# GpSimd weight products in four parts, and four early row normalisations on ScalarE instead of VectorE

## The chip, the cores and the metric

One core of one Trainium2 chip. The metric is the device time of one launch in microseconds, the median of the runs shown; lower is better.

## What is computed

Two layers on x (32 batches of 256 rows of 512 numbers), with a context of the same shape. The first works on a layer norm of x, three products with 256x256 weights and a grouped normalisation; the second is a gated feed-forward layer of width 1408 whose inputs and weights are rounded to 4-bit floating point in blocks of 16.

```python
def fp4_quant_dequant(x):                      # blocks of 16 along the last dim
    scale = max(max|x| of the block / 6, 1e-12)
    q = _GRID[searchsorted(_MID, |x / scale|)] * sign(x) * scale

x = x + xattn(layernorm(x), ctx, ctx, Wt, Wp, Wg, Wz, gamma, beta)
xn = fp4_quant_dequant(layernorm(x))
gate, y = xn @ fp4(w_gate).T, xn @ fp4(w_up).T
x = x + fp4_quant_dequant(silu(gate) * y) @ fp4(w_down).T
```

## The kernel before

Each batch b has two tiles of 128 rows (t = 2b + s). After a prologue, a hardware loop on every engine (`Fori(1, NB - 2)`) handles one batch per turn; the last batches are written out. Each engine executes its own list of instructions in the order in which the builder's functions are called, and engines meet only through semaphores. So an instruction that waits holds everything that its engine has queued behind it. Nothing but these lists, written out by hand, sets the order.

The prologue rounds the three feed-forward weights. A weight is four chunks of 128x1408 numbers (88 blocks of 16), 12 chunks n = 0 to 11 in all. For each chunk VectorE finds block maxima (`weight_max`) and scales (`weight_scales`); GpSimd multiplies the chunk by the inverse scales (`weight_y`, L1848); ScalarE makes a rounding grain (`weight_grain`, L915); VectorE adds and takes away the grain (`weight_round`, L1470 and L1473); GpSimd multiplies by the scales (`weight_q`, L1856). TensorE then transposes the chunk in 34 sets (`turn_weights`, L597), ScalarE copies each as float16 (`weights_hi`, L938), TensorE forms the remainder (`turn_again`, L605 and L607), ScalarE copies that (`weights_lo`, L944).

Woven into this are batches 0 and 1. `ln1(b)` on GpSimd makes the inverse deviations of layer norm 1, `root2(t)` that of layer norm 2. `normalise1(b, s)` (VectorE, L1223) and `normalise2(t)` (VectorE, L1272) apply them: `(x - mean) * rstd` on 128x512 numbers. ScalarE's `q_hi(b)` (L910) copies the normalised x_in as float16, GpSimd's `q_lo` (L1802) makes the remainder, SyncE's `turn_c`, `turn_q` transpose by DMA in that order, and TensorE's `gram(b)` (L500) takes both. `columns(0)` (L1810 and on) and `columns_affine(0)` (L1821 to L1831) are small GpSimd operations on the way to ScalarE's `affine` (L859), VectorE's `residual` (L1258) and `x1_mean` (L1266).

On the path of a tile's second layer, VectorE runs `x_first` (block maxima, L1205), `x_scales` (L1208, L1283), `x_y` (L1184), ScalarE `grain_x` (L915), VectorE `x_add`, `x_back`, `x_quant`, ScalarE `x_hi`, VectorE `x_lo`, and a DMA transposes. TensorE multiplies group by group (`hidden(j, s, c)`, L550), ScalarE applies silu (`silu_group`, L964), VectorE multiplies (`gated`, L1409), which raises the semaphore `h_done` by one per group.

Orders of the prologue that the steps below follow:

- VectorE, around tile 0: `weight_round(6)`, `weight_max(2, 3)`, `normalise2(0)`, `ln1_means(1)`, `residual(1, 1)`, `x_first(0)`, ..., `weight_rowmax(2)`; TensorE's `top_of_rows(2)` (L614) waits for the last.
- VectorE, around tile 1 (L1552 to L1557): `gated(0, 0, 1)`, `x_first(1)`, `x_scales(1)`, `x_y(1)`, `ln1_moments(2, 0)`, `gated(0, 0, 2)`, `h_first(0)`.
- ScalarE (L1057 to L1064): `weights_lo(21)`, `weights_hi(22)`, `silu_group(0, 0, 2)`, `weight_grain(10)`, `weights_hi(23)`, `grain_x(1)`, `weights_lo(22)`, `gram_copy(1)`.
- TensorE (L715 to L719): `hidden(0, 0, 2)`, `turn_weights(23)`, `turn_again(22)`, a wait for `h_done` of 3, `gram(1)`.

Of the kernel before, what the change touches and what calls it, by code (L numbers as in the profile page):

```python
# [17 lines left out]
P = 128  # L18
# [5 lines left out]
ALU = mybir.AluOpType  # L24
ACT = mybir.ActivationFunctionType
# [31 lines left out]
def build(nc, x, ctx_in, Wt, Wp, Wg, Wz, gamma, beta, w_gate, w_up, w_down, out):  # L57
# [19 lines left out]
    with ExitStack() as stack:  # L77
# [65 lines left out]
        ln1_rs = sb("ln1_rs", [P, HT, 2])  # L143
        u_sb = sb("u_sb", [P, HT, D])
# [81 lines left out]
        q_norm = sem("q_norm")  # L226
        q_hi_done = sem("q_hi_done")
# [589 lines left out]
        def _(act):  # L817
# [141 lines left out]

            def silu_group(j, s, c):  # L960
                act.wait_ge(gu_done, GROUPS * j + c + 1)
                at_least(act, h_done, GROUPS * j + c - 1)
                a, b = SPANS[c]
                nc.scalar.activation(silu[:, (s + c) % 2, 0:b - a], pairs[:, pair_of(j, s, c), 0, 0:b - a], ACT.Silu,  # L964
                                     scale=w_unit[:, 0:1]).then_inc(silu_done, 1)
# [18 lines left out]
            weight_grain(1)  # L984
            q_hi(0)
# [45 lines left out]
            weights_hi(13)  # L1031
            grain_x(0)
# [11 lines left out]
            weights_lo(17)  # L1044
            q_hi(1)
# [15 lines left out]
            weights_hi(23)  # L1061
            grain_x(1)
# [118 lines left out]
        def _(dve):  # L1181
# [38 lines left out]
            def normalise1(b, s):  # L1220
                dve.wait_ge(ln1_rstd, b + 1)
                dve.wait_ge(xc_ready, HT * b + s + 1)
                nc.vector.tensor_scalar(x_in[:, s, :], x_in[:, s, :], ln1_mv[:, s, 0:1], ln1_rs[:, s, 1:2],  # L1223
                                        ALU.subtract, ALU.mult).then_inc(q_norm, 1)
# [44 lines left out]
            def normalise2(t):  # L1269
                dve.wait_ge(ln2_rstd, t + 1)  # L1270
# [479 lines left out]
        def _(pool):  # L1750
# [22 lines left out]
            def ln1(b):  # L1773
# [6 lines left out]
                inverse_root(ln1_rs[:, :, 1], ln1_rs[:, :, 0], HT, b + 1, ln1_shrunk, ln1_rstd)  # L1780

# [51 lines left out]
            def root2(t):  # L1833
                pool.wait_ge(ln2_mean, t + 1)
                nc.gpsimd.tensor_tensor(ln2_rs[:, 0:1], ln2_mv[:, 1:2], eps_col[:, 0:1], ALU.add).then_inc(ln2_eps, 1)  # L1835
                inverse_root(ln2_rs[:, 1:2], ln2_rs[:, 0:1], 1, t + 1, ln2_eps, ln2_rstd)

            def weight_y(n):
# [4 lines left out]
                if n % 2 == 0:  # L1843
# [4 lines left out]
                nc.gpsimd.tensor_tensor(blocks(staged(m, c * H, H)), blocks(staged(m, c * H, H)), over_block(rinv),  # L1848
                                        ALU.mult).then_inc(w_y_done, 1)

            def weight_q(n):
# [4 lines left out]
                nc.gpsimd.tensor_tensor(blocks(staged(m, c * H, H)), blocks(staged(m, c * H, H)),  # L1856
                                        over_block(w_scale[m % 2][:, c * HB:(c + 1) * HB]), ALU.mult).then_inc(w_q_done, 1)
# [105 lines left out]
```

## Time and profile before

| | |
|---|---|
| median of 3 runs | 1741.44 us (1740.36 to 1741.53) |
| span of the profiled execution, first to last instruction | 1739.4 us |
| TensorE busy | 1682.5 us, 97% |
| VectorE busy | 1518.6 us, 87% |
| ScalarE busy | 825.6 us, 47% |
| GpSimd busy | 707.2 us, 41% |

The profile gives the span of its execution and no other time of it; the median lies 2.0 us above that span. In the profile PE is TensorE's matmuls, PEld its weight loads, DVE is VectorE, ACT is ScalarE, POOL is GpSimd, SP is SyncE. A busy time includes time in which a started instruction is held up, so an instruction that is longer than its like of the same shape has waited inside its duration. L numbers are lines of the kernel.

### The profile page before, as it was taken

Reading aid. Unit: us, or ns where it says so; the run is one execution under the profiler, and the core shown is the slowest. Engines: PE = TensorE matmul, PEld = TensorE weight load, DVE = VectorE, ACT = ScalarE, POOL = GpSimd, SP = SyncE. Lnnn points to the kernel's source line nnn. Section 1 sums busy time; section 2 is a strip of 40 time slices with the busy share of each in tenths; the row PEclk is TensorE's granted clock in tenths of the full one; section 3 lists DMA queues with packets and bytes.
Section 4 is the critical chain, followed back from the end, with each engine's and each line's share of the span. In section 5 each row is a group of like instructions: output and inputs, shape, how many; then the busy total and the mean of one; then the engine's idle time right before and its main releaser. Section 6 shows DMA issues by size and latency. Waiting matters only on the chain.

```text
span 1739.4 us, 27808 instructions
## 1 busy us (share of the span) xinstructions
PE 1682.5 (97%) x8723; PEld 922.4 (53%) x8723; DVE 1518.6 (87%) x2577; ACT 825.6 (47%) x1472; POOL 707.2 (41%) x879
## 2 busy tenths in 40 slices
PE   2789999999999999999999999999999999999999
PEld 1666555555555555555555555555555555555544
DVE  8987888889888888988888898888888988888887
ACT  3656545444445454444554444454544444545322
POOL 6865333334444333444433334443333444433310
PEclk9999999999999999999999999999999999999999
DMA  8123334334344434343434434333434444333321
GB/s 257 34 43 66 88 89 105 88 91 97 78 94 91 94 87 99 89 96 79 93 89 94 98 83 106 75 87 90 104 87 92 96 81 93 91 92 87 76 52 47
DMA packets 412150, 155.86 MB, mean 90 GB/s; under 512 B 383200, under 2 KB 384480, under 8 KB 412128
## 3 DMA queue, kind: packets, MB, share of 16 engines
q1 hardware_dynamic: 396352, 125.17, 33.7%
q10 hardware_dynamic: 15776, 30.41, 5.4%
q8 instruction: 12, 0.20, 0.0%
q14 instruction: 10, 0.08, 0.0%
HBM read 43.03 MB, written 16.78 MB: 34 GB/s over the span
## 4 chain that ended last, share of the span: by engine, by line
PE 94%; DVE 2%; ACT 2%; DMA 1%; issue 1%; POOL 0%; SPq 0%; DVEq 0%; ACTq 0%
PE pairs L550 52%; PE work L561 25%; PE work L500 5%; PE work L512 3%; PE ubank L527 2%; PE work L527 2%; PE pairs L605 1%; PE pairs L500 0%; PE pairs L597 0%; DMA hT_parts<-raw 0%; DMA raw<-in_L_ffn_w_gate 0%; DVE w_rinv L1205 0%; DVE x_in L1223 0%; PE pairs L607 0%; PE pairs L580 0%
## 5 line engine op out<-in xcount | busy, mean ns | idle before, releaser
L550 PE MATMUL pairs<-w_gate_hi,xT_parts 128*128 128x512 f16 (+1 forms) x1536 | 555.4, 362 | 1.8 <-DMA xT_parts<-raw 1.5
L550 PE MATMUL pairs<-w_up_hi,xT_parts 128*128 128x512 f16 (+1 forms) x1536 | 554.7, 361 | 0.0
L561 PE MATMUL work<-w_parts,hT_parts 128*128 128x512 f16 x2079 | 458.9, 379 | 0.9 <-DMA hT_parts<-raw 0.9
L561 PEld LDWEIGHTS work<-w_parts,hT_parts 128*128 128x128 f16 x2079 | 203.5, 99 | 236.1 <-issue 1.1
L550 PE MATMUL pairs<-w_up_lo,xT_parts 128*128 128x512 f16 (+1 forms) x768 | 277.5, 361 | 0.0
L550 PE MATMUL pairs<-w_gate_lo,xT_parts 128*128 128x512 f16 (+1 forms) x768 | 277.4, 361 | 0.0
L550 PEld LDWEIGHTS pairs<-w_gate_hi,xT_parts 128*128 128x128 f16 x1536 | 152.7, 99 | 163.2 <-issue 15.1
L550 PEld LDWEIGHTS pairs<-w_up_hi,xT_parts 128*128 128x128 f16 x1536 | 150.3, 98 | 146.5
L964 ACT ACTIVATE early<-pairs,w_unit 128x512 f32<-128x512 f32 (+1 forms) x192 | 124.9, 651 | 166.3 <-PE pairs L550 166.3
L873 ACT CAST raw<-hq 128x704 f16<-128x704 f32 x126 | 98.1, 779 | 179.5 <-DVE hq L1201 178.7
L1409 DVE SCALAR_TENSOR_TENSOR h<-pairs,w_unit,early 128x512 f32<-128x512 f32 (+1 forms) x192 | 135.0, 703 | 39.9 <-ACT early L964 34.6
L915 ACT ACTIVATE wm<-h 128x1408 bf16<-128x1408 f32 (+2 forms) x65 | 87.1, 1341 | 166.5 <-DVE h L1184 166.5
L1786 POOL TENSOR_TENSOR xc<-x_in,c_in 128x512 f32<-128x512 f32 x64 | 88.8, 1387 | 176.6 <-DVE x L1258 176.6
L1835 POOL TENSOR_TENSOR ln_rs<-ln_mv,eps_col 128x1 f32<-128x1 f32 x64 | 59.2, 925 | 215.3 <-DVE ln_mv L1266 215.3
L1810 POOL TENSOR_TENSOR att<-rowst,grp 128x2 f32<-128x2 f32 x32 | 14.0, 436 | 280.6 <-DVE grp L1245 280.6
L1201 DVE SCALAR_TENSOR_TENSOR hq<-h,h_unit 128x704 f32<-128x704 f32 (+1 forms) x129 | 111.1, 882 | 5.5
L550 PEld LDWEIGHTS pairs<-w_gate_lo,xT_parts 128*128 128x128 f16 x768 | 75.1, 98 | 77.1
L550 PEld LDWEIGHTS pairs<-w_up_lo,xT_parts 128*128 128x128 f16 x768 | 75.1, 98 | 77.0
L1349 DVE TENSOR_TENSOR raw<-hq,raw 128x704 f16<-128x704 f32 x126 | 109.3, 887 | 1.6
L1205 DVE TENSOR_REDUCE h_amax<-h 128x88 f32<-128x1408 f32 (+1 forms) x66 | 104.0, 1575 | 2.2
L1184 DVE SCALAR_TENSOR_TENSOR h<-h,h_rinv 128x1408 f32<-128x1408 f32 (+1 forms) x66 | 104.1, 1577 | 0.1
L1197 DVE SCALAR_TENSOR_TENSOR h<-wm,h 128x1408 f32<-128x1408 bf16 (+2 forms) x65 | 102.7, 1580 | 1.2
(193 smaller groups left out, 2803.6 us busy)
## 6 DMA issues: line engine op xcount, KB each, us to landing
out<-raw SPq DMA_DIRECT2D x64, 256.0 KB, 2.1
c_in<-in_ctx ACTq DMA_DIRECT2D x29, 512.0 KB, 3.8
x_in<-in_x ACTq DMA_DIRECT2D x29, 512.0 KB, 5.3
raw<-in_L_ffn_w_down SPq DMA_DIRECT2D x2, 1408.0 KB, 8.9
raw<-in_L_ffn_w_gate SPq DMA_DIRECT2D x2, 1280.0 KB, 8.3
w_parts<-in_L_ffn_w_up SPq DMA_DIRECT2D x2, 1280.0 KB, 9.4
x_in<-in_x SPq DMA_DIRECT2D x3, 512.0 KB, 3.7
c_in<-in_ctx SPq DMA_DIRECT2D x3, 512.0 KB, 4.7
```

The source lines that it names most:

```text
L550: mm = pe.matmul(pairs[:, pair, n, 0:b - a], xT[s][part][:, k, :], w1[n][wpart][:, k, a:b], start=(k == 0 and part == 0 and wpart == 0), s ...
L561: mm = pe.matmul(obank[:, :], hT[part][:, k, :], w2[wpart][:, k, :], start=(k == 0 and part == 0 and wpart == 0), stop=(k == KH - 1 and pa ...
L873: nc.scalar.copy(hq_parts[:, 0, a:b], hq[:, a:b]).then_inc(h_hi_done, 1)
L915: nc.scalar.activation(m, y, ACT.Abs, scale=GRAIN).then_inc(done, 1)
L964: nc.scalar.activation(silu[:, (s + c) % 2, 0:b - a], pairs[:, pair_of(j, s, c), 0, 0:b - a], ACT.Silu, scale=w_unit[:, 0:1]).then_inc(sil ...
L1184: nc.vector.scalar_tensor_tensor(out=blocks(y), in0=blocks(src), scalar=SNAP_BELOW, in1=over_block(rinv), op0=ALU.mult, op1=ALU.mult).then ...
L1197: nc.vector.scalar_tensor_tensor(out=y, in0=m, scalar=GRAIN, in1=y, op0=ALU.max, op1=ALU.subtract).then_inc(done, 1)
L1201: nc.vector.scalar_tensor_tensor(out=blocks(q_out), in0=blocks(y), scalar=-factor, in1=over_block(scale), op0=ALU.mult, op1=ALU.mult).then ...
L1205: nc.vector.tensor_reduce(dst, blocks(src), AX_X, ALU.max, apply_absolute_value=True).then_inc(done, 1)
L1349: nc.vector.tensor_tensor(hq_parts[:, 1, a:b], hq[:, a:b], hq_parts[:, 0, a:b], ALU.subtract).then_inc(h_lo_done, 1)
L1409: nc.vector.scalar_tensor_tensor(out=h[:, a:b], in0=pairs[:, pair_of(j, s, c), 1, 0:b - a], scalar=w_unit[:, 1:2], in1=silu[:, (s + c) % 2 ...
L1786: nc.gpsimd.tensor_tensor(xc[:, s, :], x_in[:, s, :], c_in[:, s, :], ALU.add).then_inc(xc_ready, 1)
```

## The change

Two edits, both in the prologue. `weight_y` and `weight_q` issue each product as four instructions of 22 blocks (352 columns); only the last raises the semaphore. And for batches 0 and 1, tiles 0 and 1, the normalisations leave VectorE: GpSimd makes nm = -mean * rstd in two small operations behind the inverse deviation, and ScalarE computes `rstd * x + nm`. On VectorE the first later normalisation of each kind waits for the semaphore counts that ScalarE raised. The loop's instructions are the same.

```diff
+            def early_normalise1(b, s):
+                act.wait_ge(ln1_shift, 2 * b + 2)
+                act.wait_ge(xc_ready, HT * b + s + 1)
+                nc.scalar.activation(x_in[:, s, :], x_in[:, s, :], ACT.Identity, scale=ln1_rs[:, s, 1:2],
+                                     bias=ln1_nm[:, s:s + 1]).then_inc(q_norm, 1)
+            def early_normalise2(t):
+                act.wait_ge(ln2_shift, 2 * t + 2)
+                act.wait_ge(x1_ready, t + 1)
+                at_least(act, xq_ready, t)
+                nc.scalar.activation(xn[:, :], x1[:, t % 4, :], ACT.Identity, scale=ln2_rs[:, 1:2],
+                                     bias=ln2_nm[:, 0:1]).then_inc(xn_ready, 1)
...
             weight_grain(1)
+            early_normalise1(0, 0)
+            early_normalise1(0, 1)
             q_hi(0)
...
             weights_hi(13)
+            early_normalise2(0)
             grain_x(0)
...
             weights_lo(17)
+            early_normalise1(1, 0)
+            early_normalise1(1, 1)
             q_hi(1)
...
             silu_group(0, 0, 2)
             weight_grain(10)
             weights_hi(23)
+            early_normalise2(1)
             grain_x(1)
...
             def normalise1(b, s):
+                if isinstance(b, int) and b < EARLY:
+                    return
+                if isinstance(b, int) and b == EARLY:
+                    dve.wait_ge(q_norm, HT * EARLY)
...
             def normalise2(t):
+                if isinstance(t, int) and t < EARLY:
+                    return
+                if isinstance(t, int) and t == EARLY:
+                    dve.wait_ge(xn_ready, EARLY)
...
                 inverse_root(ln2_rs[:, 1:2], ln2_rs[:, 0:1], 1, t + 1, ln2_eps, ln2_rstd)
+                if isinstance(t, int) and t < EARLY:
+                    pool.wait_ge(ln2_rstd, t + 1)
+                    at_least(pool, xn_ready, t)
+                    nc.gpsimd.tensor_tensor(ln2_nm[:, :], ln2_mv[:, 0:1], ln2_rs[:, 1:2], ALU.mult).then_inc(ln2_shift, 1)
+                    pool.wait_ge(ln2_shift, 2 * t + 1)
+                    nc.gpsimd.tensor_scalar(ln2_nm[:, :], ln2_nm[:, :], -1.0, None, ALU.mult).then_inc(ln2_shift, 1)
+            QUARTERS = [(q * HB // 4, (q + 1) * HB // 4) for q in range(4)]
...
-                nc.gpsimd.tensor_tensor(blocks(staged(m, c * H, H)), blocks(staged(m, c * H, H)), over_block(rinv),
-                                        ALU.mult).then_inc(w_y_done, 1)
+                for a, b in QUARTERS:
+                    part = blocks(staged(m, c * H, H))[:, a:b]
+                    made = nc.gpsimd.tensor_tensor(part, part, over_block(rinv[:, a:b]), ALU.mult)
+                made.then_inc(w_y_done, 1)
```

`ln1` has the same two nm operations as `root2`, and `weight_q` the same four parts as `weight_y`.

## Rows read from the trace of the kernel before

**Rows 1.** The page: busy times of the engines, us (share of the span) x instructions.

```profile
PE 1682.5 (97%) x8723; PEld 922.4 (53%) x8723; DVE 1518.6 (87%) x2577; ACT 825.6 (47%) x1472; POOL 707.2 (41%) x879
```

**Rows 2.** Windows: us, busy (x count) of PE, PEld, DVE, ACT, POOL, PEclk, DMA, GB/s.

```profile
90.00:91.00 1.00, 0.00 (x1) 0.03 (x2) 1.00 (x4) 1.00 (x3) 0.00 (x0) 0.84 0.00 0
91.00:92.00 1.00, 1.00 (x5) 0.57 (x6) 0.96 (x2) 0.50 (x2) 0.86 (x2) 0.50 0.00 0
...
94.00:95.00 1.00, 1.00 (x10) 0.92 (x9) 0.61 (x2) 0.47 (x1) 0.78 (x4) 0.95 0.00 0
...
180.00:280.00 100.00, 99.84 (x513) 53.23 (x512) 86.55 (x153) 46.33 (x84) 37.67 (x51) 1.00 0.41 91
```

**Rows 3.** VectorE's timeline: start, us, what (idle before, releaser), to 106 us.

```profile
18.47 2.37 DVE L1223 TENSOR_SCALAR x_in<-x_in,ln_mv,ln_rs 128x512 f32<-128x512 f32 x1
...
23.09 0.53 DVE L1223 TENSOR_SCALAR x_in<-x_in,ln_mv,ln_rs 128x512 f32<-128x512 f32 x1
...
24.04 2.46 DVE L1189 TENSOR_SCALAR c_norm<-c_norm 128x2 uint32<-128x2 uint32 x1
...
66.10 2.27 DVE L1208 TENSOR_SCALAR w_scale<-w_rinv 128x176 f32<-128x176 f32 x1
...
80.83 2.92 DVE L1272 TENSOR_SCALAR xn<-x,ln_mv,ln_rs 128x512 f32<-128x512 f32 x1
...
83.83 2.92 DVE L1258 TENSOR_TENSOR x<-v_sb,xc 128x512 f32<-128x512 f32 x1
86.67 0.67 DVE L1205 TENSOR_REDUCE x_amax<-xn 128x32 f32<-128x512 f32 x1
...
101.72 3.27 DVE L1223 TENSOR_SCALAR x_in<-x_in,ln_mv,ln_rs 128x512 f32<-128x512 f32 x2
```

**Rows 4.** GpSimd's timeline, same columns.

```profile
16.74 1.27 POOL L1786 TENSOR_TENSOR xc<-x_in,c_in 128x512 f32<-128x512 f32 x1
...
34.30 2.58 POOL L1856 TENSOR_TENSOR raw<-raw,w_scale 128x1408 f32<-128x1408 f32 x1
...
55.58 3.63 POOL L1848 TENSOR_TENSOR w_parts<-w_parts,w_rinv 128x1408 f32<-128x1408 f32 x1
59.42 0.20 POOL L1810 TENSOR_TENSOR att<-rowst,grp 128x2 f32<-128x2 f32 x1 [0.21 <-DVE grp L1245]
...
60.04 0.20 POOL L1815 TENSOR_TENSOR att<-att 128x2 f32<-128x2 f32 x1
60.19 0.20 POOL L1816 TENSOR_TENSOR att<-att,gb 128x2 f32<-128x2 f32 x1
```

**Rows 5.** ScalarE's timeline, same columns, to 106 us.

```profile
64.88 0.81 ACT L859 ACTIVATE v_sb<-u_sb,att 128x512 f32<-128x512 f32 x1 [0.26 <-POOL att L1831]
...
71.90 0.59 ACT L951 ACTIVATE w_scale<-w_scale,w_gain 128x352 f32<-128x352 f32 x1 [0.76 <-DVE w_gain L1463]
...
85.36 0.61 ACT L938 CAST w_up_hi<-pairs 128x512 f16<-128x512 f32 x1
...
105.02 1.04 ACT L910 CAST q_parts<-x_in 128x1024 f16<-128x1024 f32 x1 [3.11 <-DVE x_in L1223]
```

**Rows 6.** TensorE's timeline, same columns.

```profile
40.56 5.28 PE L500 MATMUL pairs<-qT,cT 128*128 128x256 f16 x24 [1.67 <-DMA qT<-q_parts]
...
91.00 0.58 PE L614 MATMUL ubank<-ident,w_max 128*1 128x128 f32 x2 [3.16 <-issue]
...
109.57 1.16 PE L605 MATMUL pairs<-ident,w_parts 128*128 128x128 f32 x8 [1.33 <-ACT w_up_hi L938]
...
124.99 2.78 PE L500 MATMUL pairs<-qT,cT 128*128 128x256 f16 x24
```

**Rows 7.** VectorE's timeline around the block maxima of tile 1, same columns.

```profile
117.55 0.68 DVE L1205 TENSOR_REDUCE x_amax<-xn 128x32 f32<-128x512 f32 x1
...
124.25 0.62 DVE L1409 SCALAR_TENSOR_TENSOR h<-pairs,w_unit,early 128x384 f32<-128x384 f32 x1 [1.05 <-ACT early L964]
```

**Rows 8.** ScalarE's timeline around set 23, same columns.

```profile
125.39 0.58 ACT L938 CAST w_parts<-pairs 128x512 f16<-128x512 f32 x1
```

More of the change, by code:

```diff
@@ L143, in build @@
         ln1_rs = sb("ln1_rs", [P, HT, 2])
+        ln1_nm = sb("ln1_nm", [P, HT])
+        ln2_nm = sb("ln2_nm", [P, 1])
+        EARLY = 2
         u_sb = sb("u_sb", [P, HT, D])
@@ L226, in build @@
         q_norm = sem("q_norm")
+        ln1_shift = sem("ln1_shift")
+        ln2_shift = sem("ln2_shift")
         q_hi_done = sem("q_hi_done")
@@ L1780, in ln1 @@
                 inverse_root(ln1_rs[:, :, 1], ln1_rs[:, :, 0], HT, b + 1, ln1_shrunk, ln1_rstd)
+                if isinstance(b, int) and b < EARLY:
+                    pool.wait_ge(ln1_rstd, b + 1)
+                    nc.gpsimd.tensor_tensor(ln1_nm[:, :], ln1_mv[:, :, 0], ln1_rs[:, :, 1], ALU.mult).then_inc(ln1_shift, 1)
+                    pool.wait_ge(ln1_shift, 2 * b + 1)
+                    nc.gpsimd.tensor_scalar(ln1_nm[:, :], ln1_nm[:, :], -1.0, None, ALU.mult).then_inc(ln1_shift, 1)
             def add_ctx(b, s):
@@ L1855, in weight_q @@
                 pool.wait_ge(w_r_done, n + 1)
-                nc.gpsimd.tensor_tensor(blocks(staged(m, c * H, H)), blocks(staged(m, c * H, H)),
-                                        over_block(w_scale[m % 2][:, c * HB:(c + 1) * HB]), ALU.mult).then_inc(w_q_done, 1)
+                scale = w_scale[m % 2][:, c * HB:(c + 1) * HB]
+                for a, b in QUARTERS:
+                    part = blocks(staged(m, c * H, H))[:, a:b]
+                    made = nc.gpsimd.tensor_tensor(part, part, over_block(scale[:, a:b]), ALU.mult)
+                made.then_inc(w_q_done, 1)
             ln1(0)
```

## The prediction

> **What bounds the kernel now.** I read the page first: TensorE is busy 97% of the span [rows 1]. Then the windows by stage: from 180 us on TensorE is busy 99.84 us of 100 [rows 2], and its own work is the same before and after. So nothing that happens elsewhere in the loop can show, and what remains is a question about the prologue: how much later or earlier does TensorE get through its fixed list there. From about 100 us on it is nearly full, so every microsecond of shift or new idle time that it has at 125 us stays to the end. The first 125 us I read engine by engine in the timelines, looking at each instruction that is longer than its like, and at each idle gap of TensorE.
>
> **What the quarters remove.** VectorE operations are held up inside their duration while GpSimd is in a wide product. The normalisation of 128x512 takes 0.53 us free and 2.37 us held; a 128x2 operation took 2.46 us; the residual 2.92 us [rows 3]. Each ends where a GpSimd instruction ends, so the wait is for the rest of that instruction, at most the 2.58 us of a product [rows 4]. With quarters it is at most some 0.8 us: a held VectorE step gains up to 1.8 us.
>
> **What the quarters add.** No row shows a quarter. Small GpSimd operations start 0.15 us apart (60.04, 60.19) [rows 4]; with that as the fixed part, three more starts add 3 x 0.15 = 0.45 us a product. The ends: nothing (the same elements and operands, so no gain), and 1.5 us, if the line through 512 columns (1.27 us) and 1408 columns (2.58 us) is taken as the rule: 1.46 ns a column, so 0.52 us fixed, less a little overlap, times three. The two rows have different operands (one repeats a scale over 16 columns), so I take 0.45, which rests on a row that measures a start alone. The Trainium skill (GPSIMD Engine Reference, section Performance versus the Vector engine) gives 4497 ns for a two-input operation of 2048 columns; with the 512-column row that is a fixed part of 0.2 us, an estimate that speaks for the same choice, and would make the addition 0.6.
>
> **The way to 75 us.** Three steps.
> (1) Removing normalise1(0, 0) lets VectorE run earlier at 20.8, and the 128x2 operation at 24.04 (which ScalarE's context copies wait for) loses about 1.8 of its 2.3 us wait; against it stand two products on GpSimd ahead of its operand (+0.9), and two normalisations now in ScalarE's queue ahead of q_hi(0), at 0.8 us each by v_sb, the same shape and form [rows 5], start to start 0.72, so 1.45. GpSimd's context remainder bounds next. I make the first gram, at 40.56 [rows 6], 1.0 earlier. SyncE issues turn_c first and turn_q behind it, as before; both come earlier alike.
> (2) From 34.30 to 59.21 GpSimd has no gap, seven products among other work, and columns(0) starts at 59.42, 0.21 after its operand [rows 4]: GpSimd and the attention chain arrive together. Seven times 0.45 is 3.15; less the 1.0 of (1), columns(0) starts 2.0 later. VectorE's locks cost GpSimd the same as before, only at other places. The affine chain loses part of one lock, so v_sb at 64.88 is 1.7 later.
> (3) ScalarE had 0.76 idle before scale_all(1) at 71.90, waiting for VectorE [rows 5]; VectorE's scale step at 66.10, 2.27 us long, waited most of that [rows 3], and is about 1.9 earlier, so that wait goes and ScalarE is late next: 1.7 - 0.76 = 0.9 later. TensorE resumes after it 0.9 later. So VectorE's gain is not cashed here.
>
> **75 to 110 us.** normalise2(0) leaves VectorE (2.92 us, 80.83), the residual's wait shrinks (2.92, 83.83) [rows 3]: VectorE is ready for x_first(0) some 7 us early. But its operand now comes from ScalarE behind weights_hi(13), which ends at 85.97 [rows 5], now 0.9 later, plus 0.75: x_first(0) at 87.6 against 86.67 [rows 3]. From there to the row maximum nothing was held before; GpSimd's late product costs it 0.4. TensorE's next stage, at 91.00 [rows 6], is 1.35 later. The pair normalise1(1) (3.27 us) [rows 3] goes from the head of a chain: ScalarE waited 3.11 us for it before q_hi(1) at 105.02 [rows 5]. Now lo(17) ends 1.35 later, at 103.25, and two normalisations end at 104.7: 0.3 earlier. TensorE's 1.33 us gap at 109.57 [rows 6] takes up the 1.35. Shift at 110 us: 0.0. The ends: with a quarter that costs nothing, about -2.5; with 1.5 a product, +7.
> The nm pairs (two small GpSimd operations, 0.55 us with their hops, four times) cost nothing: the first is covered by GpSimd's idle time before 13.45, the others by 3 us or more between a product and TensorE's need of it. Without that cover each costs 0.55.
>
> **Tile 1: a new wait on TensorE.** This is the step I weigh most. VectorE ran x_first(1) at 117.55 and five operations on, at 124.25, gated(0, 0, 2) [rows 7]; TensorE's gram(1) waits for that one and started at 124.99 [rows 6]. After the change x_first(1) needs early_normalise2(1), which stands on ScalarE behind silu_group(0, 0, 2), weight_grain(10) and weights_hi(23); the last was at 125.39, ending 125.97 [rows 8]. ScalarE cannot take it earlier: silu_group(0, 0, 2) waits for hidden(0, 0, 2), weights_hi(23) for set 23 behind that. So: 125.9 + 0.8 (normalise) + 0.7 (x_first) + 0.2 + 0.35 (scales) + 0.63 (x_y) + 0.6 (ln1_moments) + 0.62 (gated) = 129.8, and 0.5 for meetings with GpSimd's quarters: 130.3. In VectorE's queue h_first(0), x_add(1) and weight_round(10) wait behind it too. TensorE has nothing else to do: gram(1) and all behind it stand 130.3 - 125.0 = 5.3 us (4.9 to 6.0).
> **The clock.** TensorE fell idle at 87.84; in the window from 90 us its granted clock was 0.84, then 0.50 (the 1.2 GHz level), and 0.95 in that from 94 [rows 2]. A stall of 5.3 us is longer than that one of 3.16. Half clock cost some 1.5 us there (three windows at half), and the same gram took 5.28 us at 40.56 and 2.78 at 124.99 [rows 6], which is 2.5. I take 2.3, ends 1.5 and 2.7.
> Behind 125 us TensorE's idle time before is 1.8 us up to the loop, in relay gaps that move with it; nothing takes the delay up.
>
> **Sum.** 0.0 + 5.3 + 2.3 = 7.6 us. Against the profiled execution: span 1739.4 + 7.6 = 1747.0; the median lies 2.0 above the span, so 1749.0 us.
>
> **The rivals.**
> (a) The held steps of VectorE were the real limit. For it: five steps in [rows 3] that were held for about 2 us each, and TensorE's idle time in the 70s and 80s. If the columns(0) chain is not late, the shift at 110 is -2.5, and without the two falls of the clock in the 70s and at 90 us (2.5 and 1.5 back) -6.5: 1741.4 - 6.5 + 7.6 = 1742.5, so 1741 to 1745. Against it: GpSimd and attention meeting at 59.4.
> (b) Faster: (a), and TensorE gets its tile-1 stall without a clock fall, and VectorE's early lead moves hidden(0, 0, 2) and set 23 up by 10 us. Mechanism: weight_rowmax(2) and with it TensorE's stage at 91.00 come 8 us earlier, 1741.4 - 8 - 3 + 5.3 = 1736. It decides where x_first(0) runs: before 81 us. The queue position behind weights_hi(13) speaks against it.
> (c) GpSimd bound: a quarter costs 0.5 us fixed, 24 products add up to 36 us, shift +7: 1756. It decides from about 0.9 us a product.
> (d) The clock stays up through the stall: 1746.7. Inside the forecast's range.
> That the change does not do what it says: quarters do not let VectorE in between. Then the gains of (1) and (3) go and the forecast moves by less than 2 us, since they are hardly cashed.
>
> **How the numbers follow.** Forecast with (d), 1745 to 1754: 0.60. (a) 0.17, (c) 0.13, (b) 0.10. About 0.2% (3.5 us) is what a measurement of this kernel can tell from no change. Slower by more, above 1744.9: the forecast, (c) and a little of (a), 0.75; same 0.17; faster 0.08. The range, 1741.5 to 1755, leaves out most of (c) and (b).
>
> **What would show it.** Products of four parts that last 2.9 to 3.2 us together; columns(0) near 61.4; x_first(0) near 87.6 behind ScalarE; x_first(1) right behind ScalarE's normalisation near 126.7; TensorE idle about 5 us before gram(1), and that gram at half clock. Wrong if TensorE has no such gap, or if it reaches hidden(0, 0, 0) more than 4 us earlier than at 102.0.

## The result, and the profile after

The changed kernel takes 1748.81 us (median of 5 runs, 1748.09 to 1752.46), the kernel before 1741.44 us beside it: a ratio of 1.0046, 95% interval 1.0035 to 1.0057. It is slower by 7.4 us; 1749.0 had been predicted. The profiled execution took 1750.26 us with a span of 1748.5 us, 9.1 us over that of before; it is 1.45 us above the median of its kernel, so what is read from its rows adds up to more than the 7.4 us.

Busy times first (columns as in [rows 1]), then windows (as in [rows 2]), then the waits of TensorE (waits for: us in total, times, longest us).

```profile
PE 1686.3 (96%) x8723; PEld 923.4 (53%) x8723; DVE 1497.8 (86%) x2571; ACT 829.9 (47%) x1478; POOL 699.2 (40%) x959
```

```profile
65.00:66.00 1.00, 1.00 (x5) 0.91 (x4) 1.00 (x1) 0.35 (x1) 0.84 (x3) 0.50 0.00 0
...
94.00:95.00 1.00, 1.00 (x6) 1.00 (x6) 0.29 (x2) 0.34 (x1) 0.91 (x3) 0.50 0.00 0
...
129.00:130.00 1.00, 0.00 (x0) 0.00 (x0) 1.00 (x3) 0.65 (x2) 0.00 (x0) 0.74 0.00 0
132.00:133.00 1.00, 1.00 (x6) 0.70 (x5) 0.97 (x4) 0.00 (x0) 0.00 (x0) 0.50 0.00 0
180.00:280.00 100.00, 99.84 (x513) 53.68 (x512) 86.20 (x147) 47.98 (x86) 37.11 (x52) 1.00 0.40 90
```

```profile
PE pairs L505 <- DVE h L1443: 5.1, 1, 5.1
...
PE ubank L619 <- issue: 3.2, 1, 3.2
PE ubank L546 <- POOL att L1852: 2.2, 1, 2.2
```

VectorE lost 20.8 us of busy time (1518.6 to 1497.8) and GpSimd 8.0, and the kernel is slower: busy time was not what bound it. The loop is as full as before (99.84 of 100 us from 180 us on, as in [rows 2]). Two waits of TensorE are new: 5.1 us for VectorE's h (L1443), ahead of gram(1), and 2.2 us for GpSimd's att (a small tile of `columns(0)`), ahead of `group_spread(0)`, TensorE's two small matmuls on it. Behind both the granted clock is 0.50, at 65 and at 132 us. Now the engines, in the order of the prediction's steps: GpSimd, VectorE, ScalarE, TensorE (start, us, what, idle before and releaser).

```profile
18.58 3.01 POOL L1897 TENSOR_TENSOR raw<-raw,w_rinv 128x352 f32<-128x352 f32 x4
...
61.17 0.20 POOL L1849 TENSOR_TENSOR att<-rowst,grp 128x2 f32<-128x2 f32 x1
```

```profile
23.82 0.29 DVE L1215 TENSOR_SCALAR c_norm<-c_norm 128x2 uint32<-128x2 uint32 x1 [0.50 <-POOL c_norm L1805]
...
66.42 0.73 DVE L1234 TENSOR_SCALAR w_scale<-w_rinv 128x176 f32<-128x176 f32 x1
...
87.74 0.69 DVE L1231 TENSOR_REDUCE x_amax<-xn 128x32 f32<-128x512 f32 x1 [8.90 <-ACT xn L977]
...
126.93 0.69 DVE L1231 TENSOR_REDUCE x_amax<-xn 128x32 f32<-128x512 f32 x1 [8.50 <-ACT xn L977]
...
129.84 0.59 DVE L1443 SCALAR_TENSOR_TENSOR h<-pairs,w_unit,early 128x384 f32<-128x384 f32 x1
```

```profile
86.86 0.85 ACT L977 ACTIVATE xn<-x,ln_nm,ln_rs 128x512 f32<-128x512 f32 x1
...
104.53 1.04 ACT L915 CAST q_parts<-x_in 128x1024 f16<-128x1024 f32 x1
...
126.08 0.82 ACT L977 ACTIVATE xn<-x,ln_nm,ln_rs 128x512 f32<-128x512 f32 x1
```

```profile
39.86 4.86 PE L505 MATMUL pairs<-qT,cT 128*128 128x256 f16 x24
...
61.89 0.38 PE L546 MATMUL ubank<-att,gmean 128*128 128x2 f32 x2 [2.19 <-POOL att L1852]
...
69.07 1.16 PE L610 MATMUL pairs<-ident,raw 128*128 128x128 f32 x8 [0.68 <-ACT w_gate_hi L943]
...
77.01 0.63 PE L602 MATMUL pairs<-ident,raw 128*128 128x128 f32 x4 [3.65 <-ACT w_gate_lo L949]
...
92.09 0.59 PE L619 MATMUL ubank<-ident,w_max 128*1 128x128 f32 x2 [3.22 <-issue]
...
109.80 1.16 PE L610 MATMUL pairs<-ident,w_parts 128*128 128x128 f32 x8 [0.38 <-ACT w_up_hi L943]
...
130.50 5.30 PE L505 MATMUL pairs<-qT,cT 128*128 128x256 f16 x24 [5.12 <-DVE h L1443]
```

How to read them beside [rows 3 to 8]. The quarters do let VectorE in: c_norm's step at 23.82 takes 0.29 us instead of 2.46, w_scale's at 66.42 takes 0.73 instead of 2.27. Where nothing holds it, a product of four parts takes 3.01 us instead of 2.58, which is 0.43 more. Up to 110 us the two sides cancel: TensorE's row at 109.80 answers to the one at 109.57. Then comes tile 1: x_first(1) waits 8.5 us for ScalarE's xn, h of group 2 stands behind it in VectorE's list, gram(1) waits for h: 130.50 instead of 124.99, and 5.30 us long at half clock instead of 2.78.

To carry such a shift through the trace I use one mark for all kernels, the start of the first output product (the first matmul that multiplies hT_parts by the second weights). It is at 164.59 us before and at 172.92 us after, 8.33 later. (The expectations below give 164.75 and 173.09 for the same place, read 0.16 us further on.) The start of the last output product is 9.03 later (1720.05 and 1729.08); the rest of the span is alike.

### The profile page after: what moved, and what is told of

It is laid out like the page before. It is cut to its first block, busy times and chain, and to the rows that moved or that the text cites. A ratio compares the mean times of both kernels' runs of the same rounds, so it can differ in the third digit from the quotient of the medians.

```text
span 1748.5 us, 27890 instructions
## 1 busy us (share of the span) xinstructions
PE 1686.3 (96%) x8723; PEld 923.4 (53%) x8723; DVE 1497.8 (86%) x2571; ACT 829.9 (47%) x1478; POOL 699.2 (40%) x959
## 4 chain that ended last, share of the span: by engine, by line
PE 93%; POOL 3%; ACT 1%; DMA 1%; DVE 1%; issue 1%; SPq 0%; DVEq 0%; POOLq 0%; ACTq 0%
PE pairs L555 52%; PE work L566 25%; PE work L505 4%; PE work L517 3%; PE ubank L532 2%; PE work L532 2%; PE pairs L610 2%; POOL raw L1908 1%; POOL raw L1897 1%; PE pairs L602 1%; DMA raw<-in_L_ffn_w_gate 0%; DMA hT_parts<-raw 0%; POOL w_parts L1897 0%; PE pairs L612 0%; PE pairs L505 0%
## 5 line engine op out<-in xcount | busy, mean ns | idle before, releaser
L878 ACT CAST raw<-hq 128x704 f16<-128x704 f32 x126 | 98.1, 778 | 159.8 <-DVE hq L1227 158.0
L1443 DVE SCALAR_TENSOR_TENSOR h<-pairs,w_unit,early 128x512 f32<-128x512 f32 (+1 forms) x192 | 135.0, 703 | 39.4 <-ACT early L984 34.2
L920 ACT ACTIVATE wm<-h 128x1408 bf16<-128x1408 f32 (+2 forms) x65 | 87.1, 1341 | 166.5 <-DVE h L1210 166.5
```

The lines of the kernel that those rows point to most:

```text
L878: nc.scalar.copy(hq_parts[:, 0, a:b], hq[:, a:b]).then_inc(h_hi_done, 1)
L920: nc.scalar.activation(m, y, ACT.Abs, scale=GRAIN).then_inc(done, 1)
L1443: nc.vector.scalar_tensor_tensor(out=h[:, a:b], in0=pairs[:, pair_of(j, s, c), 1, 0:b - a], scalar=w_unit[:, 1:2], in1=silu[:, (s + c) % 2 ...
```

## The experiments

The kernels of the experiments start from the changed kernel, where nothing else is said. This table has the marks of all of them, in us: the start of the attention columns on GpSimd (columns), of x_first(0) on VectorE, of gram(1) and its length, of the first and the last output product, then the median. The medians of before were 1741.45 to 1741.57 beside them. Starts are of one profiled execution, medians of 5 to 11. Two executions with the same instructions up to a mark can have it 1 to 3 us apart (changed, e3, e5 and e12 run the same code up to 90 us, and have x_first(0) between 86.03 and 89.30), so small differences between marks show nothing by themselves.

| kernel | columns | x_first(0) | gram(1), length | first output | last output | median |
|---|---|---|---|---|---|---|
| before | 59.42 | 86.67 | 124.99, 2.78 | 164.59 | 1720.05 | 1741.4 |
| changed | 61.17 | 87.74 | 130.50, 5.30 | 172.92 | 1729.08 | 1748.8 |
| e1 quarters only | 61.54 | 80.88 | 120.90, 2.78 | 161.97 | 1717.85 | 1739.0 |
| e2 norms only | 57.05 | 83.07 | 127.08, 4.46 | 168.91 | 1725.01 | 1746.7 |
| e3 tile 1 on VectorE | 61.20 | 86.17 | 125.05, 2.78 | 165.35 | 1723.86 | 1746.6 |
| e4 gap filled | 61.30 | 87.90 | 131.59, 2.78 | 171.52 | 1729.20 | 1749.3 |
| e5 gated first | 61.06 | 86.03 | 124.89, 2.78 | 168.58 | 1727.49 | 1748.5 |
| e6 tile 1 early | 61.14 | 87.69 | 126.77, 2.78 | 168.05 | 1725.67 | 1745.9 |
| e7 both early | 61.10 | 79.89 | 122.67, 2.78 | 162.61 | 1718.99 | 1741.2 |
| e8 both early, wholes to 61 us | 58.20 | 77.51 | 120.22, 2.78 | 160.16 | 1717.02 | 1738.3 |
| e9 both early, all whole | 57.12 | 78.41 | 119.19, 2.78 | 158.79 | 1716.48 | 1740.5 |
| e10 before, gap at 88 filled | 59.83 | 87.07 | 125.25, 2.78 | 165.17 | 1721.38 | 1743.2 |
| e11 e8, two gaps filled | 58.01 | 75.90 | 118.14, 2.78 | 158.77 | 1714.84 | 1737.6 |
| e12 e3 and one ScalarE copy | 61.28 | 89.30 | 126.70, 2.78 | 167.78 | 1724.12 | 1745.3 |

**The two halves of the change.** e1 has the quarters and no row normalisation on ScalarE (all six calls are out):

```
-        EARLY = 2
+        EARLY = 0
-            early_normalise1(0, 0)
...
-            early_normalise2(1)
```

> The four-part products alone, all four normalisations back on VectorE. My theory (the loss is tile 1's normalisation standing behind weights_hi(23) on ScalarE): no gap before gram(1), which runs in about 2.8 us; columns(0) still starts near 61.3, since the extra starts on GpSimd are still there; but x_first(0) no longer waits for ScalarE and runs near 80, so TensorE's gap at 91 goes. 1737 us (1734 to 1741). Rival (the extra GpSimd starts cost the time): it stays slower than before, 1745 or more.

Measured: 1739.03 us (1738.54 to 1741.41), ratio 0.9987, interval 0.9978 to 0.9996. e2 has the normalisations and whole products, in weight_y and in weight_q:

```
-                for a, b in QUARTERS:
+                for a, b in [(0, HB)]:
```

> The four moved normalisations alone, each product one instruction as before. My theory: columns(0) starts near 59, but x_first(1) still starts at about 127 and TensorE stands 5 us before gram(1), which then takes about 5.3 us at half clock: 1747.5 us (1745 to 1750). Rival (GpSimd's extra starts): no slower than before, 1741 or less.

Measured: 1746.65 us (1744.50 to 1747.41), ratio 1.0024, interval 1.0014 to 1.0034. VectorE's and TensorE's timelines, e1:

```profile
80.88 0.67 DVE L1225 TENSOR_REDUCE x_amax<-xn 128x32 f32<-128x512 f32 x1
...
142.82 0.38 PE L546 MATMUL ubank<-att,gmean 128*128 128x2 f32 x2 [0.77 <-POOL att L1842]
```

and e2:

```profile
83.07 0.69 DVE L1231 TENSOR_REDUCE x_amax<-xn 128x32 f32<-128x512 f32 x1 [4.42 <-ACT xn L977]
...
127.08 4.46 PE L505 MATMUL pairs<-qT,cT 128*128 128x256 f16 x24 [4.75 <-DVE h L1443]
```

The quarters alone gain 2.5 us, the normalisations alone lose 5.1, both lose 7.4: together they are 4.8 worse than the sum of the two (2.6). The rows suggest why. With VectorE still loaded (e1), the columns are 2.1 late, but x_first(0), which needs only VectorE, runs 5.8 earlier, and gram(1) 4.1 earlier; 1.5 of this is given back by the first output product, 0.77 of it where GpSimd's late att makes TensorE wait (142.82). With VectorE relieved (e2), GpSimd alone paces the columns, they are 2.4 early, and quarters make them late: 61.17 in the changed kernel against 57.05. That the whole of the 4.8 comes this way is argued; no run separates it. The gap before gram(1) is in e2 (4.75 us) and not in e1.

**What makes the gap.** e3 gives tile 1's normalisation back to VectorE; e4 keeps it where it is and fills TensorE's gap with products nobody reads; e5 changes only VectorE's order.

```
+        EARLY2 = 1
...
-            early_normalise2(1)
...
-                if isinstance(t, int) and t < EARLY:
+                if isinstance(t, int) and t < EARLY2:
```

> The changed kernel with tile 1's layer norm 2 (normalise2(1)) back on VectorE, all else as changed. My theory: x_first(1) near 118.5, gram(1) near 125.2 without a gap and at full clock: the 5.3 + 2.5 us go, 1741 us (1739 to 1743.5). Rival (several small delays of the change add up, GpSimd first): more than half of the 7.4 us stays, 1745 or more.

Measured: 1746.59 us (1744.72 to 1747.90), ratio 1.0027, interval 1.0018 to 1.0037.

```
             turn_again(22)
+            unit_read(2)
+            for r in range(23):
+                pe.matmul(ubank[:, :], w1[0][0][:, 0, 0:P], w1[0][0][:, 0, 0:D], start=True, stop=True)
             pe.wait_ge(h_done, 3)
             gram(1)
```

> The changed kernel with 23 matmuls of 128x512 without use put in front of TensorE's wait for gated(0, 0, 2), some 5.0 us of work in a 5.1 us gap: the wait keeps its length and the clock should not fall. If half clock behind the stall costs the 2.5 us that I took: gram(1) in 2.8 us instead of 5.3, and 1746.2 us (1745 to 1747.5). If the clock costs nothing, because other waits hide it: 1748.8, unchanged.

Measured: 1749.28 us (1748.37 to 1750.38), ratio 1.0042, interval 1.0028 to 1.0056.

```
+            ln1_moments(2, 0)
+            gated(0, 0, 2)
             x_first(1)
             x_scales(1)
             x_y(1)
-            ln1_moments(2, 0)
-            gated(0, 0, 2)
```

> Only the order on VectorE changes: ln1_moments(2, 0) and gated(0, 0, 2) stand ahead of x_first(1), which still waits for the normalisation at the place it has on ScalarE behind weights_hi(23). Theory (the stall of 5.1 us ahead of gram(1) comes from what is queued behind the waiting instruction on VectorE): TensorE starts gram(1) within 0.5 us of the end of hidden(0, 0, 2), about 125.4, at full clock and 2.8 us long. But x_first(1) still cannot start before 126.9 and now h_first(0), x_add(1), weight_round(10) and with them weight_q(10) and TensorE's turns of set 28 stay late, so up to 3 us of the 8.3 us are lost again between gram(1) and the first output product, which I expect at 168 to 170 (173.09 in the changed kernel, 164.75 before). Time 1744.5 to 1746. Rival (the normalisation itself is what is late, whatever VectorE does first): the same idle time comes back in one piece behind gram(1), the first output product at 172 to 173, 1748.5 us.

Measured: 1748.51 us (1746.75 to 1749.95, and one run of 2547.48 far outside, which is in the median), ratio 1.0037, interval 1.0024 to 1.0050. TensorE's timelines, of e4:

```profile
126.62 5.13 PE L725 MATMUL ubank<-w_gate_hi 128*128 128x512 f16 x23
131.59 2.78 PE L505 MATMUL pairs<-qT,cT 128*128 128x256 f16 x24
```

and of e5:

```profile
124.89 2.78 PE L505 MATMUL pairs<-qT,cT 128*128 128x256 f16 x24
...
129.91 0.52 PE L602 MATMUL pairs<-ident,raw 128*128 128x128 f32 x3 [1.13 <-ACT w_parts L949]
...
142.62 0.66 PE L602 MATMUL pairs<-ident,raw 128*128 128x128 f32 x4 [1.14 <-POOL raw L1908]
```

At gram(1) all three did as the theory said. e3 has no gap and starts it at 125.05 (124.99 before). e4 has the same 2.78 us as at full clock, so the fall of the clock costs 2.5 us at the gram alone. e5 has no gap either: what stood behind the waiting instruction on VectorE was what TensorE missed. e5 then loses 4.1 us piece by piece up to the first output product, since x_first(1) and all behind it are still late; its mark, 168.58, is within the 168 to 170 expected.

The medians are another matter, and three expectations of them failed (1741, 1746.2, at most 1746); e5's median is that of its rival, though its mark is not. e4's mark is only 1.4 earlier than that of the changed kernel, since its gram(1) started 1.1 later: the clock behind the gap at 92 us came back at 98.1 us and not at 95.4 as there, and TensorE's row of 109.80 stands at 111.21. The rows behind the mark name the other pieces. In e3 a turn of the loop takes longer. These are group_means in two turns, 25 turns apart, in the kernel before and in e3:

```profile
290.25 0.28 PE L535 MATMUL ubank<-rowst,gmean 128*128 128x6 f32 x2
...
1548.60 0.28 PE L535 MATMUL ubank<-rowst,gmean 128*128 128x6 f32 x2
```

```profile
291.36 0.28 PE L541 MATMUL ubank<-rowst,gmean 128*128 128x6 f32 x2
...
1551.55 0.28 PE L541 MATMUL ubank<-rowst,gmean 128*128 128x6 f32 x2
```

That is 50.334 us a turn before and 50.408 in e3, with the same instructions in the loop: over 29 turns 2.1 us. And the last turns, where TensorE waits for the DMA transpose of the last-but-one tile, differ between the kernels: it landed in 3.1 us before and in 3.7 us in the changed kernel, e3 and e4; TensorE's rows, before and changed:

```profile
1684.39 0.39 PE L550 MATMUL pairs<-w_gate_hi,xT_parts 128*128 128x512 f16 x1 [1.46 <-DMA xT_parts<-raw]
```

```profile
1693.43 0.39 PE L555 MATMUL pairs<-w_gate_hi,xT_parts 128*128 128x512 f16 x1 [2.17 <-DMA xT_parts<-raw]
```

The longer wait of e4 (3.06 us) is not explained by this landing. In e4, e5, e6 and e9 the wait (3.06, 2.17, 2.25 and 2.16 us) is followed by half clock, which costs 1.6 to 1.7 us more: 15.9 to 16.0 us from there to the next output product instead of 14.27. In the changed kernel the clock stays at 1.00 behind the same 2.17 us, and in e11 behind 3.06. A window of e5 (us, PE busy, PEclk, DMA, GB/s):

```profile
1691.00:1692.00 1.00, 1.00 (x4) 0.50 0.10 37
```

In e5 a DMA transpose in the loop's first turn comes 1.1 us late as well; with 0.7 for the landing and 1.7 for the clock this is all of the 3.5 us that e5 has more than before between its first and last output product.

**The place in ScalarE's queue.** e6 moves tile 1's normalisation up (the lower half of the diff), e7 that of tile 0 too:

```
             weights_lo(9)
+            early_normalise2(0)
...
             weights_hi(13)
-            early_normalise2(0)
...
             weights_lo(16)
+            early_normalise2(1)
...
             weights_hi(23)
-            early_normalise2(1)
```

> early_normalise2(1) alone moves on ScalarE, from behind weights_hi(23) to right behind weights_lo(16), some 25 us earlier in the queue, where its operand is ready. Theory (its place in ScalarE's queue is the whole cost of tile 1): no idle time of TensorE ahead of gram(1), which starts near 125.4 at full clock (2.8 us); the first output product at 165.0 (164.75 before, 173.09 changed), 8 us earlier than in the changed kernel; time 1741 us, 1739.5 to 1743.5 with what the loop's period and the tail differ between kernels. Rival (it waits for something else too, the xn buffer that tile 0 still uses, or VectorE is late for another reason): the gap stays, at 2 us or more, and the time is 1744 or more.

Measured: 1745.87 us (1742.60 to 1746.96), ratio 1.0021, interval 1.0012 to 1.0030.

> As the kernel with tile 1's normalisation moved behind weights_lo(16), and tile 0's moved too, from behind weights_hi(13) to right behind weights_lo(9) on ScalarE. Theory (rival (b) of the prediction: where x_first(0) runs decides when TensorE gets its stage at 91): x_first(0) at 80 to 81 instead of 87.7, as with the quarters alone (80.88), TensorE's idle 3.2 us at 91 and the half clock behind it gone, hidden(0, 0, 0) near 98.5, first output product at 160 to 162; time 1737 to 1739. Rival (TensorE's resume at 77.0, 2 us late because of the later attention columns, eats it): first output product at 164 to 165, 1741.

Measured: 1741.17 us (1739.01 to 1742.48), ratio 0.9996, interval 0.9987 to 1.0005. They are faster than the changed kernel by 2.9 and 7.6 us. In e6 the gap is gone, and gram(1) ends at 129.55 instead of 135.80. Its median had been expected at 1741 and the profiled execution, 5.7 us over the span of before, shows three things that were not. The first is the clock behind TensorE's gap near 90 us, here in windows of e6 (us, PE busy, PEclk, DMA, GB/s), and then of the changed kernel, all engines:

```profile
96.00:97.00 1.00, 1.00 (x7) 0.50 0.00 0
97.00:98.00 1.00, 1.00 (x7) 0.65 0.00 0
```

```profile
95.00:96.00 1.00, 1.00 (x8) 0.91 (x8) 0.00 (x0) 0.29 (x1) 0.86 (x3) 0.82 0.00 0
```

The code is the same up to here and the gap nearly so (3.54 and 3.22 us), yet TensorE's clock is back at 95.4 us in the changed kernel and at 97.7 in e6. TensorE is 0.26 us later than in the changed kernel ahead of this stretch and 1.26 behind it, so the clock makes 1.0 us here; the moved normalisation, which now stands on ScalarE at 101.10, adds 0.3, and at 110 us TensorE is 1.6 us later. The second is a load of the context that takes 6.1 us to land instead of 4.1 (one line of the DMA view of each, KB and us to landing), which, with a wait of 0.45 us for GpSimd's att, makes e6's way from group_means(1) to the first output product 1.7 us longer than before:

```profile
c_in<-in_ctx SPq DMA_DIRECT2D x1, 512.0 KB, 6.1
```

```profile
c_in<-in_ctx SPq DMA_DIRECT2D x1, 512.0 KB, 4.1
```

The third is the tail, with half clock behind its wait as in e5. So the stall was worth what the sum said at the place where it stood (5.1 and 2.5), and its removal brought 2.9 us to the median. e7 nearly met its marks (x_first(0) at 79.89, first output product at 162.61 with 162 as the end of the range), but not its time (1737 to 1739); 1741.17 is what its rival gave, though not by the rival's mark of 164 to 165. The gap at 91 is gone, the rival's late columns (61.10) are not, and behind two shorter waits, 0.75 and 1.36 us, half clock stands from 105.8 to 109.2 us. e8 below has the same, from 103.7 us:

```profile
103.13 1.60 PE L610 MATMUL pairs<-ident,w_parts 128*128 128x128 f32 x8 [1.36 <-ACT w_up_hi L943]
```

**Where the columns start.** e8 is e7 with whole products between 34 and 61 us; e9 is e7 with whole products everywhere.

```
             def weight_y(n):
...
-                for a, b in QUARTERS:
+                for a, b in (QUARTERS if n < 3 or n > 5 else [(0, HB)]):
...
             def weight_q(n):
...
-                for a, b in QUARTERS:
+                for a, b in (QUARTERS if n > 3 else [(0, HB)]):
```

> As the kernel with both normalisations moved up, and the products between 34 and 61 us whole again (weight_y(3) to weight_y(5), weight_q(0) to weight_q(3)), quarters elsewhere. Theory (7 x 0.45 us of starts are what makes columns(0) late): columns(0) at 58 to 58.5 us instead of 61.2, TensorE's wait of 2.2 us for GpSimd at 61.9 gone or under 0.5, its resume at 77.0 moved to 74.5 to 75, and the first output product 1.5 to 2.5 us ahead of that of the kernel with quarters everywhere, so 158 to 160; time 1735 to 1737.5. Rival (VectorE, held by whole products in that stretch, is late by the same): columns(0) waits for VectorE at 59.5 or later and nothing is gained, time as with quarters everywhere.

Measured: 1738.25 us (1736.94 to 1739.19), ratio 0.9980, interval 0.9972 to 0.9989.

> The row normalisations on ScalarE at the early places, and every wide product of GpSimd whole: the quarters left out altogether. Theory A (the early normalisation carries the gain, and quarters matter only as GpSimd time): x_first(0) within 1 us of the 77.5 us that it had with part of the products whole, GpSimd's x + c for the second batch earlier, so ScalarE's wait of 2.4 us for it at 97.7 shrinks; first output product at 158.5 to 160.5 (160.16 there), time 1737 to 1738.5. Theory B (VectorE, held for up to 1.8 us by each whole product, needs the quarters after 61 us): x_first(0) at 79 us or later, first output product at 161.5 to 163, time 1739.5 to 1741.

Measured: 1740.51 us (1737.67 to 1741.16), ratio 0.9992, interval 0.9983 to 1.0001. VectorE's and TensorE's timelines of e9, and two windows (columns as for e6) of it:

```profile
79.11 2.60 DVE L1234 TENSOR_SCALAR x_scale<-x_amax 128x32 f32<-128x32 f32 x1
...
87.28 0.38 PE L619 MATMUL ubank<-ident,w_max 128*1 128x128 f32 x2 [3.26 <-issue]
```

```profile
87.00:88.00 1.00, 0.72 (x6) 1.00 0.00 0
88.00:89.00 1.00, 1.00 (x12) 1.00 0.00 0
```

e8 did what theory said at the columns (58.20); its first output product, 160.16, is 2.4 us before e7's and just outside the 158 to 160, and its median 0.7 us above the range. It beats both kernels. e9 splits the quarters' worth. In its profiled execution theory A holds (mark 158.79). That this is 1.4 us ahead of e8 does not show that no quarter is needed, since e8's execution had half clock from 103.7 to 107.1 us and e9's had none there. The median of e9, 1740.51, is theory B's. In its rows x_scale is held for 2.60 us by a whole product, the row maximum comes late, TensorE has its 3.26 us gap at 87 again, and in this execution the clock stayed at 1.00 behind it. That execution (1737.67, with 1.7 us of half clock in the tail) is the fastest of eleven; eight took 1739.76 to 1741.16. e8 has no such gap at 87 and spreads over 2.3 us. That the eight are those in which the clock fell is argued, not shown.

**What the clock costs.** e10 is the kernel before with its gap at 88 us filled (ahead of top_of_rows(2)), e11 is e8 with two gaps filled.

```
             unit_read(1)
+            for r in range(13):
+                pe.matmul(ubank[:, :], w1[0][0][:, 0, 0:P], w1[0][0][:, 0, 0:D], start=True, stop=True)
```

> The kernel before, with 13 matmuls of 128x512 whose results nobody reads in TensorE's gap from 87.84 to 91.00, so that it has no idle time over 0.6 us there. Theory (the half clock behind that gap costs 1.5 to 1.9 us where it lasts 3.7 us, and 3.3 where it lasts 6.5, and which of the two happens is what spreads the runs of one kernel): granted clock 1.00 from 90 to 98 us, first output product at 162.7 to 163.1 (164.59 before), median 1739.5 to 1740 with fewer runs above 1742. Rival (what follows is bound by VectorE and ScalarE, which the clock does not touch): the clock stays up and the first output product moves by less than 0.5 us, median 1741.4.

Measured: 1743.21 us (1741.95 to 1745.39), ratio 1.0014, interval 1.0005 to 1.0023. A window of it (columns as for e6) and TensorE's timeline:

```profile
90.00:91.00 1.00, 1.00 (x5) 1.00 0.00 0
```

```profile
109.83 1.16 PE L605 MATMUL pairs<-ident,w_parts 128*128 128x128 f32 x8 [2.25 <-ACT w_up_hi L940]
```

The rival held at the mark: it is 0.58 us later, and 0.4 of that stands at the columns already, ahead of the fill. The clock stays up, and TensorE just waits longer at 109.8 (2.25 us instead of the 1.33 in [rows 6]): ScalarE's work ends last there. Half clock up to 94 us costs the kernel before nothing; only what goes beyond the slack does, as in e6. The fill gained nothing and the median is 1.8 higher, which neither theory nor rival had; 1.2 of that stands in the loop's first turn, where a DMA transpose lands late, as in e5. What the fill has to do with it stays open.

```
             turn_weights(9)
+            unit_read(1)
+            for r in range(14):
+                pe.matmul(ubank[:, :], w1[0][0][:, 0, 0:P], w1[0][0][:, 0, 0:D], start=True, stop=True)
...
             turn_weights(20)
+            unit_read(2)
+            for r in range(5):
+                pe.matmul(ubank[:, :], w1[0][0][:, 0, 0:P], w1[0][0][:, 0, 0:D], start=True, stop=True)
```

> The kernel with both normalisations moved up and whole products from 34 to 61 us, with useless matmuls in two gaps of TensorE: 14 ahead of its resume at 72.94, 5 ahead of 103.13. Theory: full clock behind both, 1.0 us won at 73 (the six operations there at half clock), of which ScalarE takes most back, and 1.5 at 103; first output product at 158.2 to 159.2 (160.16), time 1736.5 to 1737.3. Rival (TensorE is not what binds at 73 to 100 us, and the fall at 103 comes all the same, from the 0.57 us wait before it): first output product at 159.8 to 160.4, time 1738.

Measured: 1737.58 us (1736.02 to 1739.05), ratio 0.9980, interval 0.9971 to 0.9989.

```profile
72.74 0.63 PE L602 MATMUL pairs<-ident,raw 128*128 128x128 f32 x4 [0.63 <-ACT w_gate_lo L955]
```

Full clock all the way and the mark at 158.77, as expected; the median is 0.3 us above the range. Its interval overlaps with that of e8, so a gain over e8 is not shown.

**The turn of the loop.** e12 is e3 with one ScalarE instruction more ahead of the loop:

```
+        pad_tile = sb("pad_tile", [P, P])
...
             weights_hi(23)
+            act.wait_ge(ident_made, 2)
+            nc.scalar.activation(pad_tile[:, :], ident[:, :], ACT.Identity)
             grain_x(1)
```

> As the kernel with tile 1's normalisation back on VectorE, whose loop turn took 50.407 us instead of 50.334, plus one ScalarE copy of 128x128 into a tile that nobody reads, at the place where that normalisation stood in the changed kernel. The loop's instructions are the same in all kernels. Theory (where ScalarE's instruction stream lies, one instruction earlier or later, sets how long a semaphore takes to release its x_hi copy): the loop turn is 50.33 to 50.35 us again, and the median 2 us lower, 1744 to 1745. Rival (the loop turn follows from how far apart the engines are when they enter the loop): the turn stays at 50.40 to 50.41 us and the median at 1746.5. First output product at 165 to 166.5 in both.

Measured: 1745.34 us (1742.39 to 1745.81), ratio 1.0016, interval 1.0007 to 1.0026.

```profile
293.45 0.28 PE L542 MATMUL ubank<-rowst,gmean 128*128 128x6 f32 x2
...
1552.00 0.28 PE L542 MATMUL ubank<-rowst,gmean 128*128 128x6 f32 x2
```

The turn is 50.34 us again (25 turns in 1258.55), which takes 1.9 us out of the loop (29 turns by 0.066). Mark and median missed their ranges (165 to 166.5, 1744 to 1745). The median fell by 1.25 us only; in the profiled execution the first output product is 2.4 later than e3's, whose code is the same up to 125 us: its granted clock was 0.66 on average from 60 to 70 us. e3 and e12 were profiled once each, so that the turn belongs to the kernel, and not to the execution, is not shown. In all the other kernels it is 50.32 to 50.35 us. Whether it is, if so, the place of the instructions, as the theory has it, or when ScalarE enters the loop, one added copy can't tell apart, since it changes both.

## Why the prediction was right

The time was right (1749.0 against 1748.8), and so was the step that carried it, tile 1's normalisation. That the two times agree to 0.2 us is luck: the rows of the profiled execution add up to 8.3 us at the first output product where the sum had 7.6, and that execution lies 1.45 us above the median. Point by point:

- **Quarters**: 0.45 us a product predicted, 0.43 measured (3.01 against 2.58 in [rows 4]); the row of the small starts was the right one to go by. The estimate from the Trainium skill's figure (GPSIMD Engine Reference, Performance versus the Vector engine) was 0.6, a little high.
- **Held VectorE steps**: gains of 1.5 to 2.2 us, with up to 1.8 predicted from [rows 3]. The Trainium skill says of the pair of ports that VectorE and GpSimd share (SBUF — State Buffer, SBUF: two separate sides) that whoever starts first has it for the whole instruction. The traces agree: w_scale's step at 66.42 loses less than one part of 0.75 us now, and x_scale's in e9, with whole products, takes 2.60 us.
- **(1), (2)**: gram(0) 0.7 earlier (1.0 predicted), columns at 61.17 (61.4 predicted).
- **(3)**: here a step failed. TensorE resumes 1.98 later, not 0.9. I followed ScalarE's chain and took TensorE as a guest in it; but TensorE's own wait of 2.19 us for att was new, and behind it the clock fell to half from 64.7 to 68 us. TensorE was 1.20 late at 62.9 and 2.85 late at 69; the wait for w_gain that went away took 0.9 of this back. I had priced the fall of the clock for the 5 us stall and not looked for shorter ones. How much of the 1.98 is the clock, e3 and e5 show, which have the same instructions up to there and late columns too (61.20, 61.06), but a wait for att of 1.10 and 1.22 us and no fall behind it. TensorE's rows of e3:

```profile
67.45 1.16 PE L611 MATMUL pairs<-ident,raw 128*128 128x128 f32 x8 [0.67 <-ACT w_gate_hi L944]
...
75.40 0.74 PE L603 MATMUL pairs<-ident,raw 128*128 128x128 f32 x4 [3.65 <-ACT w_gate_lo L950]
```

  They resume at 75.40 and 75.26, 0.4 and 0.2 us later than before. So columns that are 1.8 us late, with the wait for w_gain gone, cost 0.2 to 0.4 us here, less than the 0.9 of the sum, and the half clock costs 1.6 (69.07 against 67.45, and 77.01 against 75.40).
- **75 to 110 us**: x_first(0) 87.74 (87.6), the stage at 92.09 (+1.09; 1.35 predicted), the shift at 110 us +0.23 (0.0 predicted). That (3) was 1.1 off did not matter, and this is luck: by 84.33 TensorE is 1.03 late (83.30 before), since behind the gap in the 70s half clock stood from 78.3 to 81.4 us, and before from 75.0 to 80.4. The gap at 109.57 took up most of the rest. In e4, with the same instructions, the row of 109.80 is 1.64 later than before, so 0.2 is not what every execution has.
- **Tile 1**: gram(1) at 130.50 (130.3), behind x_first(1) at 126.93 and ScalarE's normalisation at 126.08. e5 and e6 show both halves of the reason: VectorE's order, and the place in ScalarE's queue.
- **The clock**: 2.3 predicted, 2.8 measured: TensorE is 5.51 us late at the start of gram(1) and 8.32 behind it, at 137.04. 2.52 of this is the gram's own length, and e4, with the clock up, has it back.
- **Sum**: 7.6 predicted, 8.33 measured at the first output product. The term that was too small is the clock's (2.8 for 2.3). The median differs by 7.4, the profiled spans by 9.1; 0.7 of the latter is the tail.
- **"Nothing that happens elsewhere in the loop can show"**: this fell. In the changed kernel the loop's turn bears it out (50.332 us, before 50.334), but the one profiled execution of e3 does not, with 0.074 us a turn more.
- **"Nothing takes the delay up"**: held for the delay, 8.33 us from 148 us to the tail. It does not hold the other way round: e1 gave back 1.5 of 4.1 us; e5 was 8.1 ahead of the changed kernel at gram(1)'s end and 4.3 at the first output product.

Of the rivals, (a) had its mechanism right for a kernel that this is not: in e1 the held steps were the limit. (b) named the point that decides, x_first(0) before 81 us, and e7 and e8 show it, though the gain over before was 3.3 us in e8 and not 5. (c) had the price wrong: three more starts cost 0.43 us together, 0.14 each, not 0.5. But that GpSimd's time can be what binds is so: on top of the moved normalisations (e2) the quarters cost 2.2 us of the median and 4.0 at the first output product. (d) did not happen.

## What to carry to other kernels

An instruction that is moved to a queue with slack takes the place of its neighbours there: what counts is when the instruction ahead of it ends, and who waits behind its consumer. Here one normalisation of 0.82 us behind weights_hi(23) stopped TensorE for 5.1 us and cost it its clock, and some 20 calls further up in ScalarE's list it did neither (e6). Splitting a holder of a shared resource pays where the held engine is late, and costs where the holder is; look at both for each stretch, not once for the kernel: here quarters gain 2.5 us alone (e1) and cost 2.2 on top of e2. And a gain of 1 or 2 us ahead of a loop has to be measured with many runs, since idle gaps, clock and DMA landings add as much from one execution to the next.

## What the runs showed of the hardware

- TensorE's clock fell behind an idle time of 2.19 us (changed kernel, 61.9 us) and did not fall behind one of 3.26 us (e9, 87 us). Behind the same 2.17 us near the end it fell in e5 and stayed in the changed kernel. Shorter waits had a fall behind them too: 1.19 and 0.68 us in e3 (at 50.0 and 51.4 us, granted clock 0.50 from 52), 0.57 and 1.36 us in e8 (at 100.7 and 103.1), 0.64 us and then this row's in e12. At the two places of e12, e3 waited 0.86 and 1.10 us and had no fall:

```profile
62.01 0.38 PE L548 MATMUL ubank<-att,gmean 128*128 128x2 f32 x2 [1.34 <-POOL att L1855]
```

- Half clock lasted from 91.9 to 95.4 us in the changed kernel and from 90.9 to 97.7 in e6, with the same code and nearly the same gap. Of the ramp at the start of a kernel the Trainium skill says that it is run-variable (TensorE: Matmul & The Clock Gate, Part 1, What's actually happening); the runs agree for a gap in the middle of one. The difference was worth 1.0 us there, and half clock or none at 64 us was worth 1.6 (changed kernel against e3).
- In the profiled executions the same loop took 50.32 to 50.35 us a turn in thirteen kernels and 50.41 in one (e3), whose instructions in the loop are the same. The cause stays open.
- The same DMA transpose of the tail took 3.1 us in some kernels and 3.7 to 3.9 in others, and the same 512 KB load of the context, near 145 us, 3.7 to 6.1 us.
